# Householder columns: the corrections' place among the matrix-vector products, and VectorE's order, chosen by the number of live blocks

## The chip, the cores and the metric

The program runs on 1 core of one Trainium2 chip. The metric is the device time of one execution in microseconds (us); lower is better. Engines are named as the profile names them: PE is TensorE's matmul, PEld TensorE's weight load, DVE is VectorE, ACT is ScalarE, SP is SyncE.

## What is computed

The reference is a chain of eight residual layers over x. One of them, the third graph layer, needs the eigenvectors of a 512 x 512 symmetric matrix:

```python
def _L2_gnn_ref(features, A, W1, b1, W2, b2):
    deg = jnp.sum(A, axis=0) + jnp.sum(A, axis=1) - jnp.diagonal(A)
    d_inv_sqrt = jnp.where(deg > 0, jax.lax.rsqrt(deg), 0.0)
    L = jnp.diag(deg) - A
    L_norm = d_inv_sqrt[:, None] * L * d_inv_sqrt[None, :]
    _, U = jnp.linalg.eigh(L_norm)
    ...
x = x + _L2_gnn_ref(_layernorm(x, axis=-1), adj, ...)
```

The matrix depends on `adj` alone, so the kernel does this part first: `tridiagonalize` takes the symmetrised matrix to tridiagonal form by 512 Householder reflections, one column after the other. All of the change lies in it. Everything after it (`eigenvectors` and the eight layers) is untouched.

## The kernel before

The 512 columns are cut into 4 phases of 128. In phase `ph` the first `ph` blocks of 128 rows are done, so `L = NB - ph` blocks are live: 4, 3, 2, then 1. All small vectors have 128 partitions and `L` elements in each. A phase has 8 panels of 16 columns (`PW = 16`; `j` counts the columns of a panel). Inside a panel the matrix `A` is not updated; instead each new column gets corrections from the reflectors of the panel so far (`VW`, 2j vectors). At a panel's end two transposes and one rank-32 product on TensorE update `A`, and `A` is split anew into three bf16 parts (`parts`).

One column is a chain between VectorE and TensorE, with a little of ScalarE. With the lines of the profile:

- VectorE writes the new column `x` (L590) and the panel's vector pair (`update_column`, L478).
- `norm_parts`: two sums of products go to TensorE (`part`, L318 and L326, or L328 at one block); `x` is split into three bf16 numbers (R1, L329; R2, L334, which signals `xb_in`); the mask for "is anything nonzero" is multiplied (L331).
- `pair_sums`: the products of the column with the panel's vectors (L414) and their sum over blocks (L421, signals `sums_in`).
- TensorE adds the parts over partitions (`norm_sum`, L680, into `tot`); then it waits for `xb_in` and computes the matrix-vector products `ax` (L702: `3*L*L` matmuls of 128 x 128 by 3, `L` groups of `3*L`), and among them the `corrections` (L691, into `sr`), which wait for `sums_in`. Their place is before group `L // 2`; at one block it is behind the group.
- ScalarE takes the root (L645). VectorE makes the signed norm (L342, L344, L347, `sign_norm` L359), multiplies the corrections out (`spread`, L426) and sums them (`corrected`, L441), then waits for `ax_out`.
- Behind `ax_out`: `sum_parts` (L452), `reflector` (L368), `shifted_column` (L447), `leading` (L375), `product_column` (L458), `inverses` (L382), and the two dot products `jc` and `jd` (L576, L577, or L580, L582 at one block), which go to TensorE (`dots`, L714). While TensorE adds them, VectorE does `inverse_c` (L389), `scales` (L396, L397), `base_column` (L464), `scaled_x` (L404) and `masked_base` (L471). With `dots` the next `x` is written.

VectorE's order is the program's order: each engine takes its instructions one by one, and a wait in front of one holds all behind it. The first column of a panel (j = 0) does its norm ahead, while TensorE updates `A`.

`wide_step` in the listing is never run: it needs `L > 4`, and `L` is at most 4. All columns go through `narrow_step`.

The place of the corrections, in TensorE's program:

```python
for m in range(ph, NB):
    if L > 1 and m == ph + L // 2:
        corrections()
    for b in range(ph, NB):
        for n, A_part in enumerate(parts):
            ins = nc.tensor.matmul(ax[:, m, 0:3], ...)
```

Of the kernel before, what the change touches and what calls it, by code (L numbers as in the profile page):

```python
# [9 lines left out]
ALU = mybir.AluOpType  # L10
ACT = mybir.ActivationFunctionType
AX = mybir.AxisListType
# [63 lines left out]
def tridiagonalize(nc, C, adj_d, adjT_d, V, G, ER, DR, also):  # L76
# [10 lines left out]
    with ExitStack() as ctx:  # L87
# [32 lines left out]
        xax = sb("xax", [P, NB, 3])  # L120
# [3 lines left out]
        prod = sb("prod", [P, 2 + 2 * PAIR, NB])  # L124
        prod2 = sb("prod2", [P, 2, 2, NB, 1 + PAIR])
        sums, srs = sb("sums", [P, 2 + 2 * PAIR]), sb("srs", [P, 2 + 2 * PAIR])
        cross, ab = sb("cross", [P, 2 * PAIR]), sb("ab", [P, 4])
        part, part2 = sb("part", [P, 4]), sb("part2", [P, 1])
# [9 lines left out]
        turned, dots, dots2 = M[0:PAIR, NB - 2, :], M[:, 0, 0:2], M[:, 1, 0:1]  # L138
# [5 lines left out]
        part2_in, dots2_out, mask0, acol0 = sem("part2_in"), sem("dots2_out"), sem("mask0"), sem("acol0")  # L144
# [146 lines left out]
        for ph in range(NB):  # L291
# [3 lines left out]
            split_sums = L > 4  # L295
            SUM0 = 2 if split_sums else 1
            ahead = lambda panel: panel in panels and panel > panels[0]
            with nc.Block() as block:
                @block.vector
                def _(dve):  # L300
# [10 lines left out]
                    def norm_parts(done, j):  # L311
# [3 lines left out]
                        R_1, R_2 = XM[:, q, live, R1], XM[:, q, live, R2]  # L315
# [13 lines left out]
                        V_.tensor_tensor(R_1, x, XB[:, q, live, 2 * XC + 1], ALU.subtract).then_inc(ch, 1)  # L329
                        r1_made = done.next()  # L330
                        V_.scalar_tensor_tensor(prod[:, 0, live], x, 0.0, below, ALU.not_equal, ALU.mult).then_inc(ch, 1)  # L331
                        made["nonzero"] = done.next()
                        dve.wait_ge(ch, r1_made)
                        V_.tensor_tensor(R_2, R_1, XB[:, q, live, 2 * R1 + 1], ALU.subtract).then_inc(xb_in, 1)  # L334

                    def signed_norm(done, j):
# [12 lines left out]
                        if j == 0 or split_sums:  # L349
                            sign_norm(done, j, twice)  # L350
# [55 lines left out]

                    def pair_sums(done, j):

                        q, J = j % 2, 2 * j
                        first, x, below = column(q)  # L410
                        xm = XM[:, q, live, :]
                        if j > 0:
                            dve.wait_ge(ch, made["w"])
                            V_.tensor_tensor(  # L414
                                prod[:, SUM0:SUM0 + 2 * J, live].rearrange("p (h j) b -> p h j b", h=2),
                                VW[:, live, 0:J].rearrange("p b j -> p j b").unsqueeze(1).broadcast_to([P, 2, J, L]),
                                xm[:, :, FIRST:XC + 1].rearrange("p b h -> p h b").unsqueeze(2).broadcast_to([P, 2, J, L]),
                                ALU.mult).then_inc(ch, 1)
                            made["nonzero"] = done.next()
                        dve.wait_ge(ch, made["nonzero"])  # L420
                        V_.tensor_reduce(sums[:, 0:SUM0 + 2 * J], prod[:, 0:SUM0 + 2 * J, live], AX.X, ALU.add).then_inc(sums_in, 1)  # L421

                    def spread(done, j, sums_of):

                        q, J = j % 2, 2 * j
                        V_.tensor_tensor(  # L426
                            prod2[:, q, :, live, 1:1 + J],
                            VW[:, live, PAIR:PAIR + J].unsqueeze(1).broadcast_to([P, 2, L, J]),
                            sums_of.rearrange("p (h j) -> p h j", h=2).unsqueeze(2).broadcast_to([P, 2, L, J]),
                            ALU.mult).then_inc(ch, 1)  # L430
                        made["spread"] = done.next()
# [54 lines left out]
                    def wide_step(done, j, k):  # L486

                        q, J = j % 2, 2 * j
                        first, x, below = column(q)
                        if j > 0:  # L490
                            dve.wait_ge(dots2_out, j)
                            update_column(done, j - 1, dots2)
                        V_.tensor_tensor(prod[:, 1, live], x, A[:, live, k + 1], ALU.mult).then_inc(ch, 1)
                        made["nonzero"] = done.next()
                        pair_sums(done, j)
                        if j > 0 or not made["ahead"]:
                            signed_norm(done, j)
                            leading(done, j)
                            reflector(done, j)
                            inverses(done, j)  # L500
                        dve.wait_ge(sr_out, j + 1)
                        V_.tensor_copy(srs[:, 0:2 + 2 * J], sr[:, 0:2 + 2 * J]).then_inc(ch, 1)
                        held = done.next()
                        dve.wait_ge(ch, held)
                        if j > 0:
                            spread(done, j, srs[:, 2:2 + 2 * J])
                        inverse_c(done, j, srs[:, 0:1])
                        if j > 0:
                            V_.tensor_tensor(
                                cross[:, 0:2 * J].rearrange("p (h i t) -> p h i t", h=2, t=2),  # L510
                                srs[:, 2:2 + 2 * J].rearrange("p (h i t) -> p h i t", h=2, t=2)[:, :, :, ::-1],
# [2949 lines left out]
```

## Time and profile before

| what | us |
|---|---|
| median of 3 runs | 6996.93 (6984.87 to 6997.0) |
| the profiled execution | 6991.48 |
| its span, first to last instruction | 6989.8 |
| first `x` to last `x` of phase L = 4 (128 columns) | 50.14 to 745.30 |
| of L = 3 | 763.83 to 1366.81 |
| of L = 2 | 1380.78 to 1930.51 |
| of L = 1 | 1941.09 to 2457.84 |

The four phases fill the first 35% of the span. On the page PE is busy for 72% of the whole, DVE for 66%, ACT for 33%, but that is a mean over stages of different kinds. The page's chain of what ended last names only the very end (X, L2018). For the columns one reads the timeline of single columns: a line gives start, duration, engine, line, operation, out<-in and, in brackets, how long the engine had been idle and what ended that. "x24" means that so many alike instructions stand in one line.

### The profile page before, as it was taken

What the parts mean: (1) busy time and instruction counts of PE and PEld (TensorE: products, weight loads), DVE (VectorE), ACT (ScalarE), POOL (GpSimd) and SP (SyncE); (2) the same over time, 40 slices, a digit from 0 to 9 for tenths busy, and PEclk for the clock granted to TensorE, in tenths of its full rate; (3) what the DMA queues carried; (4) which work ended last, traced back from release to release, by engine and by line L of the source; (5) the groups of instructions that cost most, each with busy time, mean ns of one, the idle gap of its engine ahead of it and who ended that gap; (6) DMA issues with size and microseconds to landing.
All of it is one profiled execution on the core that took longest, in us unless ns stands there. A gap on an engine that the chain in (4) does not pass through costs nothing. (4 is left out here: it accounts for less than half of the span.)

```text
span 6989.8 us, 107601 instructions
## 1 busy us (share of the span) xinstructions
PE 5054.2 (72%) x32063; PEld 3565.7 (51%) x32063; DVE 4611.9 (66%) x27100; ACT 2308.3 (33%) x7352; POOL 17.9 (0%) x36
## 2 busy tenths in 40 slices
PE   4666555555544479988999995994474699776999
PEld 4555544444433335455666662563242477544676
DVE  7888888888888843248999998677454333424333
ACT  1222222222222234337688994110020133201333
POOL 0000000000000000000000000000000000000000
PEclk9999999999999999988999997997787799886999
DMA  0000000000000000010000000000010000000000
GB/s 37 2 2 2 2 1 1 2 1 1 1 1 1 1 20 0 0 49 7 4 6 4 6 4 8 1 1 1 1 49 1 12 0 0 9 0 13 0 0 24
DMA packets 23206, 48.04 MB, mean 7 GB/s; under 512 B 5673, under 2 KB 16322, under 8 KB 20930
## 3 DMA queue, kind: packets, MB, share of 16 engines
q1 hardware_dynamic: 22722, 42.40, 1.8%
q8 instruction: 204, 3.34, 0.2%
q14 instruction: 280, 2.29, 0.1%
HBM read 34.00 MB, written 8.39 MB: 6 GB/s over the span
## 5 line engine op out<-in xcount | busy, mean ns | idle before, releaser
L714 PE MATMUL h_M<-h_part,ones 128*128 128x2 f32 x1024 | 300.7, 363 | 585.9 <-DVE h_jd L577 422.2
L2011 DVE SCALAR_TENSOR_TENSOR f_ACC<-f_yp,f_CG,f_ACC 128x128 f32<-128x128 f32 x1024 | 288.4, 344 | 461.6 <-DVEq L2009 461.5
L702 PEld LDWEIGHTS h_ax<-h_XM,h_parts 128*128 128x128 bf16 x11520 | 529.7, 117 | 114.0 <-issue 114.0
L714 PEld LDWEIGHTS h_M<-h_part,ones 128*128 128x128 f32 x1024 | 256.7, 311 | 635.6 <-DVE h_jd L577 454.9
L680 PE MATMUL h_tot<-h_part,ones 128*128 128x2 f32 x1024 | 300.8, 363 | 378.7 <-DVE h_jb L326 291.1
L1956 PEld LDWEIGHTS f_yp<-f_W,f_hs 128*128 128x128 f32 x4096 | 490.0, 192 | 92.5 <-issue 91.8
L1890 PE MATMUL f_hp<-f_rows,f_W 128*128 128x512 f32 x1024 | 531.4, 601 | 5.1 <-ACT U L1900 3.0
L1058 ACT ACTIVATE e_XD<-e_X,e_scal 128x60 f32<-128x60 f32 x2048 | 527.6, 333 | 17.5 <-DVEq L922 15.7
L1987 ACT ACTIVATE f_hs<-f_hp,f_b 128x512 f32<-128x512 f32 x512 | 347.6, 685 | 539.6 <-ACTq L1986 539.6
L659 ACT ACTIVATE h_VW<-h_v,h_s 128x8 f32<-128x8 f32 (+3 forms) x512 | 154.8, 302 | 1122.9 <-DVE h_s L396 1122.9
L1946 PE MATMUL f_hp<-f_XT,f_W 128*128 x1024 | 483.5, 600 | 33.0 <-PEq L2240 33.0
L702 PE MATMUL h_ax<-h_XM,h_parts 128*128 128x3 bf16 x11520 | 441.2, 167 | 87.9 <-DVE h_parts L169 87.8
L1956 PE MATMUL f_yp<-f_W,f_hs 128*128 128x128 f32 x4096 | 493.5, 275 | 0.0
L680 PEld LDWEIGHTS h_tot<-h_part,ones 128*128 128x128 f32 x1024 | 256.8, 312 | 438.5 <-DVE h_jb L326 336.4
L1880 PEld LDWEIGHTS f_yp<-f_W,UT 128*128 128x128 f32 x2048 | 266.5, 194 | 188.8 <-issue 92.2
L1880 PEld LDWEIGHTS f_yp<-f_W,U 128*128 128x128 f32 x2048 | 268.5, 192 | 114.2 <-issue 93.1
L691 PE MATMUL h_sr<-h_sums,ones 128*128 128x1 f32 (+15 forms) x1024 | 320.4, 403 | 3.9
L1880 PE MATMUL f_yp<-f_W,UT 128*128 128x128 f32 x2048 | 281.0, 281 | 41.4 <-ACT UT L1900 32.2
L2577 PE MATMUL g_PG<-g_HL,g_Wih 128*128 128x256 f32 (+2 forms) x624 | 288.4, 619 | 1.0 <-DVE g_HL L2524 0.8
L645 ACT ACTIVATE h_s<-h_tot 128x1 f32<-128x1 f32 x512 | 87.8, 171 | 590.2 <-PE h_tot L680 589.6
L943 DVE SCALAR_TENSOR_TENSOR e_PB<-e_PB,e_scal,e_u 128x60 f32<-128x60 f32 x1024 | 281.2, 275 | 0.1
L947 DVE SCALAR_TENSOR_TENSOR e_PB<-e_PB,e_scal,e_u 128x60 f32<-128x60 f32 x1024 | 281.2, 275 | 0.0
(685 smaller groups left out, 10601.6 us busy)
## 6 DMA issues: line engine op xcount, KB each, us to landing
f_S<-in_f_W SPq DMA_DIRECT2D x64, 128.0 KB, 2.2
X<-in_x SPq DMA_DIRECT2D x1, 4096.0 KB, 16.3
f_W<-in_f_W SPq DMA_DIRECT2D x2, 2048.0 KB
spill<-f_xts SPq DMA_DIRECT2D x16, 256.0 KB, 2.0
f_rows<-spill SPq DMA_DIRECT2D x16, 256.0 KB, 2.6
f_W<-in_f_W SPq DMA_DIRECT2D x4, 1024.0 KB
out<-X SPq DMA_DIRECT2D x1, 4096.0 KB, 11.1
h_A<-in_adj SPq DMA_DIRECT2D x1, 1024.0 KB, 5.5
```

What stands on the lines that cost most here:

```text
L680: nc.tensor.matmul(tot[j % 2][:, 0:2], C.ones[:, :], part[:, 0:2], start=True, stop=True).then_inc(tot_out, 1)
L691: nc.tensor.matmul(sr[:, 0:n], C.ones[:, :], sums[:, 0:n], start=True, stop=True).then_inc(sr_out, 1)
L702: ins = nc.tensor.matmul(ax[:, m, 0:3], A_part[:, b, m * P:(m + 1) * P], XB[:, q, b, 2 * XC + 1:2 * R2 + 2:2], start=(b == ph and n == 0), ...
L714: nc.tensor.matmul(dots, C.ones[:, :], part[:, 2:4], start=True, stop=True).then_inc(dots_out, 1)
L1058: ins = nc.scalar.activation(XD[b][:, k, h, :], X[:, :], ACT.Identity, bias=scal[b][:, k, 2 * h:2 * h + 1])
L1880: ins = nc.tensor.matmul(self.yp[d % 3][:, 0:D], self.hs[unit % 2][:, j, i * P:(i + 1) * P], self.W2[:, unit % E * FC + j, :], start=(j == ...
L1890: nc.tensor.matmul(self.hp[s % 3][:, :], self.W1[:, e, j * P:(j + 1) * P], self.rows[:, g % 2, :], start=True, stop=True).then_inc(self.h_ ...
L1946: nc.tensor.matmul(hp[:, u % 2, c, :], W1[:, col // F, col % F:col % F + P], rows_t, start=True, stop=True).then_inc(h_full, 1)
L1956: ins = nc.tensor.matmul(yp[:, u % 2, k, :], hs[:, u % 2, c, k * P:(k + 1) * P], W2[:, u * UC + c, :], start=(c == 0), stop=(c == UC - 1))
L1987: nc.scalar.activation(hs[:, u % 2, c, :], hp[:, u % 2, c, :], func, bias=b1[:, u * UC + c:u * UC + c + 1]).then_inc(hs_full, 1)
L2011: ins = V_.scalar_tensor_tensor(ACC[:, k, :], yp[:, u % 2, k, :], CG[:, k * E + e:k * E + e + 1], ACC[:, k, :], ALU.mult, ALU.add)
L2577: ins = nc.tensor.matmul(o2, Wih[:, p - 1, gi * D:(gi + 1) * D], x, start=True, stop=(t == 0))
```

## The change

- `wide_step` and all that only it used go away, with two semaphores (`dots2_out`, `part2_in`) that were cleared at each panel's end on VectorE and TensorE.
- The corrections move: at L = 4 from behind two groups of products to behind one; at L = 3 and 2 from behind one to ahead of all; at L = 1 from behind the only one to ahead of it.
- `narrow = L <= 3` now names widths 3, 2 and 1. There VectorE makes the pair products and their sums before the third part R2 of `x`, and `reflector` stands before the wait for `ax_out`.
- At L = 4 `sign_norm` stands before the wait for the corrections; `leading`, `reflector`, `shifted_column` and `inverses` before the wait for `ax_out`; `inverse_c` before `jc` and `jd`.
- At the first column of a panel the sums are made with the norm ahead.

```diff
-            split_sums = L > 4
-            SUM0 = 2 if split_sums else 1
+            narrow = L <= 3
...
+                    def opening(done, j):
+                        norm_parts(done, j)
+                        if narrow:
+                            nonzeros(done, j)
+                            if j > 0:
+                                pair_products(done, j)
+                            first_rest(done, j)
+                            pair_sums(done, j)
+                            second_rest(done, j)
+                        else:
+                            first_rest(done, j)
+                            nonzeros(done, j)
+                            second_rest(done, j)
+                            if j > 0:
+                                pair_products(done, j)
+                            pair_sums(done, j)
...
+                    def norm_ahead(done):
+                        opening(done, 0)
+                        sign_norm(done, 0, signed_norm(done, 0))
+                        leading(done, 0)
+                        reflector(done, 0)
+                        inverses(done, 0)
...
+                        fresh = j > 0 or not made["ahead"]
+                        if fresh:
+                            opening(done, j)
                             twice = signed_norm(done, j)
+                            if not narrow or j == 0:
+                                sign_norm(done, j, twice)
                         dve.wait_ge(sr_out, j + 1)
                         if j > 0:
-                            spread(done, j, sr[:, 1:1 + 2 * J])
-                            sign_norm(done, j, twice)
+                            spread(done, j)
+                            if narrow:
+                                sign_norm(done, j, twice)
                         corrected(done, j)
-                        dve.wait_ge(ax_out, j + 1)
-                        sum_parts(done)
-                        if j > 0 or not made["ahead"]:
-                            reflector(done, j)
-                        shifted_column(done, j)
-                        if j > 0 or not made["ahead"]:
-                            leading(done, j)
-                        product_column(done)
-                        if j > 0 or not made["ahead"]:
-                            inverses(done, j)
+                        if narrow:
+                            if fresh:
+                                reflector(done, j)
+                            dve.wait_ge(ax_out, j + 1)
+                            sum_parts(done)
+                            shifted_column(done, j)
+                            if fresh:
+                                leading(done, j)
+                            product_column(done)
+                            if fresh:
+                                inverses(done, j)
+                        else:
+                            if fresh:
+                                leading(done, j)
+                                reflector(done, j)
+                            shifted_column(done, j)
+                            if fresh:
+                                inverses(done, j)
+                            dve.wait_ge(ax_out, j + 1)
+                            sum_parts(done)
+                            inverse_c(done, j, sr[:, 0:1])
+                            product_column(done)
...
-                        inverse_c(done, j, sr[:, 0:1])
+                        if narrow:
+                            inverse_c(done, j, sr[:, 0:1])
...
-                        for used in (ch, masks_in, dots_out, dots2_out, sr_out, root_out, ax_out, scaled_out, kept):
+                        for used in (ch, masks_in, dots_out, sr_out, root_out, ax_out, scaled_out, kept):
...
-                                if L > 1 and m == ph + L // 2:
+                                if m == (ph if narrow else ph + 1):
                                     corrections()
...
-                            if L == 1:
-                                corrections()
...
-                        for used in (panel_in, part_in, part2_in, sums_in, xb_in):
+                        for used in (panel_in, part_in, sums_in, xb_in):
```

`first_rest` is R1, `second_rest` is R2, `nonzeros` is L331, `pair_products` is L414 and `pair_sums` is now L421 alone.

## Rows read from the trace of the kernel before

**Rows 1.** Windows of L = 4 and L = 1: start:end, length, busy us of engines, PEclk, DMA share.

```profile
50.14:745.30 695.16, 436.64 (x6970) 374.66 (x6970) 560.33 (x4268) 148.79 (x825) 0.00 (x0) 1.00 0.01 2
1941.09:2457.84 516.75, 243.83 (x1171) 204.95 (x1171) 438.99 (x3825) 112.55 (x783) 0.00 (x0) 1.00 0.00 1
```

**Rows 2.** Timeline, one column of L = 4, j = 3.

```profile
238.90 0.86 PEld L702 LDWEIGHTS h_ax<-h_XM,h_parts 128*128 128x128 bf16 x24
239.02 0.21 DVE L421 TENSOR_REDUCE h_sums<-h_prod 128x13 f32<-128x52 f32 x1
...
239.64 0.23 DVE L347 SCALAR_TENSOR_TENSOR h_s<-h_s,h_tot 128x1 f32<-128x1 f32 x1
239.68 0.50 PEld L691 LDWEIGHTS h_sr<-h_sums,ones 128*128 128x128 f32 x2
...
239.92 0.90 PEld L702 LDWEIGHTS h_ax<-h_XM,h_parts 128*128 128x128 bf16 x24
240.13 0.78 PE L702 MATMUL h_ax<-h_XM,h_parts 128*128 128x3 bf16 x24
240.32 0.20 DVE L426 TENSOR_TENSOR h_prod<-h_VW,h_sr 128x48 f32<-128x48 f32 x1 [0.46 <-PE h_sr L691]
...
240.56 0.21 DVE L441 TENSOR_REDUCE h_zy<-h_prod 128x8 f32<-128x56 f32 x1
240.95 0.17 DVE L452 TENSOR_REDUCE h_y<-h_ax 128x4 f32<-128x12 f32 x1 [0.17 <-PE h_ax L702]
241.03 0.21 DVE L368 SCALAR_TENSOR_TENSOR h_v<-h_XM,h_s 128x4 f32<-128x4 f32 x1
241.17 0.21 DVE L447 SCALAR_TENSOR_TENSOR h_zc<-h_zy,h_s 128x4 f32<-128x4 f32 x1
...
241.61 0.16 DVE L576 SCALAR_TENSOR_TENSOR h_jc<-h_XM,h_pc 128x4 f32<-128x4 f32 x1
...
241.92 0.59 PE L714 MATMUL h_M<-h_part,ones 128*128 128x2 f32 x2 [1.01 <-DVE h_jd L577]
...
242.63 0.23 DVE L590 SCALAR_TENSOR_TENSOR h_XM<-h_vm,h_M,h_base 128x4 f32<-128x4 f32 x1
```

**Rows 3.** Timeline, one column of L = 4, j = 10.

```profile
271.68 0.33 DVE L421 TENSOR_REDUCE h_sums<-h_prod 128x41 f32<-128x164 f32 x1
...
272.12 0.50 PEld L691 LDWEIGHTS h_sr<-h_sums,ones 128*128 128x128 f32 x2
...
274.10 0.16 DVE L576 SCALAR_TENSOR_TENSOR h_jc<-h_XM,h_pc 128x4 f32<-128x4 f32 x1
```

**Rows 4.** Timeline, one column of L = 3, j = 8.

```profile
947.53 0.16 DVE L329 TENSOR_TENSOR h_XM<-h_XM 128x3 f32<-128x3 f32 x1
...
948.10 0.26 DVE L421 TENSOR_REDUCE h_sums<-h_prod 128x33 f32<-128x99 f32 x1
...
948.41 0.50 PEld L691 LDWEIGHTS h_sr<-h_sums,ones 128*128 128x128 f32 x2
...
949.55 0.16 DVE L452 TENSOR_REDUCE h_y<-h_ax 128x3 f32<-128x9 f32 x1
...
950.20 0.16 DVE L576 SCALAR_TENSOR_TENSOR h_jc<-h_XM,h_pc 128x3 f32<-128x3 f32 x1
```

**Rows 5.** Timeline, one column of L = 2, j = 15.

```profile
1577.24 0.28 DVE L421 TENSOR_REDUCE h_sums<-h_prod 128x61 f32<-128x122 f32 x1
...
1577.57 0.50 PEld L691 LDWEIGHTS h_sr<-h_sums,ones 128*128 128x128 f32 x2
```

**Rows 6.** Timeline, one column of L = 1, j = 3.

```profile
2019.26 0.23 DVE L347 SCALAR_TENSOR_TENSOR h_s<-h_s,h_tot 128x1 f32<-128x1 f32 x1
2019.46 0.17 DVE L426 TENSOR_TENSOR h_prod<-h_VW,h_sr 128x16 f32<-128x16 f32 x1
```

**Rows 7.** Timeline, the end of a panel of L = 4.

```profile
120.83 0.23 DVE L478 SCALAR_TENSOR_TENSOR h_VW<-h_VW,h_M,h_pc 128x8 f32<-128x8 f32 x1
121.68 1.41 PEld L720 LDWEIGHTS h_M<-ident,h_VW 128*32 128x32 f32 x8 [1.21 <-issue]
```

More of the change, by code:

```diff
@@ L405, in scaled_x, with pair_products, spread @@
                         made["vm"] = done.next()
-                    def pair_sums(done, j):
[L409 to L423, printed above, removed]
+                    def pair_products(done, j):
+                        J = 2 * j
+                        xm = XM[:, j % 2, live, :]
+                        dve.wait_ge(ch, made["w"])
+                        V_.tensor_tensor(
+                            prod[:, 1:1 + 2 * J, live].rearrange("p (h j) b -> p h j b", h=2),
+                            VW[:, live, 0:J].rearrange("p b j -> p j b").unsqueeze(1).broadcast_to([P, 2, J, L]),
+                            xm[:, :, FIRST:XC + 1].rearrange("p b h -> p h b").unsqueeze(2).broadcast_to([P, 2, J, L]),
+                            ALU.mult).then_inc(ch, 1)
+                        made["prod"] = done.next()
+                    def pair_sums(done, j):
+                        dve.wait_ge(ch, made["prod"])
+                        V_.tensor_reduce(sums[:, 0:1 + 4 * j], prod[:, 0:1 + 4 * j, live], AX.X, ALU.add).then_inc(sums_in, 1)
+                    def spread(done, j):
                         q, J = j % 2, 2 * j
@@ L551, in narrow_step @@
-                    def narrow_step(done, j, k):
-                        q, J = j % 2, 2 * j
-                        first, x, below = column(q)
-                        pair_sums(done, j)
-                        twice = None
-                        if j > 0 or not made["ahead"]:
+                    def opening(done, j):
[14 more added lines that the diff above has]
+                            pair_sums(done, j)
@@ L563, in narrow_step @@
                         corrected(done, j)
-                        dve.wait_ge(ax_out, j + 1)
-                        sum_parts(done)
-                        if j > 0 or not made["ahead"]:
-                            reflector(done, j)
-                        shifted_column(done, j)
-                        if j > 0 or not made["ahead"]:
-                            leading(done, j)
-                        product_column(done)
-                        if j > 0 or not made["ahead"]:
-                            inverses(done, j)
+                        if narrow:
[20 more added lines that the diff above has]
+                            product_column(done)
@@ L613, in _ @@
                         if made["ahead"]:
[L614 to L618 removed]
+                            norm_ahead(done)
                         sp = ph if panel + 1 in panels else ph + 1
```

112 lines of the change are left out of this document (23 added, 89 removed).

## Prediction

> **What bounds the kernel now.** I read the windows by phase first, then the timeline of single columns at each width and each j, and last the panel's end. The windows show what kind of stage this is: VectorE is busy for 560 of 695 us at four blocks and for 439 of 517 at one, TensorE for 437 and 244, and the granted clock is 1.00, the upper level of 2.4 GHz, in both, also where TensorE idles for half the time [rows 1]. So neither engine's total is the bound. A column is one chain that goes from VectorE to TensorE and back three times, and 512 columns stand one behind the other: 2408 of 6990 us lie there, and what a column's chain gains, the kernel gains. Nothing else runs beside it.
>
> In the column of L = 4, j = 3 the reader is to see three things [rows 2]. TensorE takes up the corrections (239.68) only when its 24 weight loads are through; the sums that they need were ready at 239.02 + 0.21 = 239.23. VectorE waits twice: 0.46 us for the corrections, and 0.17 us for the products (240.95). And behind the products there are six starts up to `jc` at 241.61, of which only `sum_parts`, `product_column` and `jc` need the products.
>
> The steps that I use, all from these rows. A short VectorE instruction starts 0.08 behind another that it doesn't need (240.95, 241.03) and 0.14 behind one with a column and a per-partition scalar (241.03, 241.17); behind a wide one it may start about 0.08 before that one's end. One that needs the result starts 0.04 after its end (240.32 + 0.20, then 240.56) [rows 2]. TensorE starts 0.05 after the VectorE instruction that it waits for (1577.24 + 0.28, then 1577.57) [rows 5]. A weight load of the products takes 0.78/24 = 0.0325, the corrections hold TensorE for 0.24 (239.68 to 239.92), and their result is used 0.64 after their start (240.32) [rows 2].
>
> **Dead code.** `wide_step` never ran, so its removal is worth nothing but one semaphore clear less per panel on each engine. VectorE's lies beside TensorE's transposes. TensorE's lies on the path: from the end of L478 (121.06) to the transposes (121.68) there are 0.62 us with five clears in them [rows 7]. Less the 0.05 of the wake-up that is 0.11 a clear at most, 0 at least; I take 0.1, since nothing else is in the gap: 32 panels, 3 us.
>
> **L = 4, early columns (j = 3).** The corrections stand behind 12 loads, so they start at 238.90 + 0.39 = 239.29 (the sums are there at 239.28), 0.39 earlier. TensorE doesn't stand, so the products end where they did, and `sum_parts` stays at 240.95. VectorE has `sign_norm` done ahead (239.64 + 0.23 + 0.04 = 239.91), so `spread` starts at 239.99, `corrected` 0.24 later at 240.23, and `leading`, `reflector`, `shifted_column`, `inverses` at 240.36, 240.44, 240.58, 240.72, all covered by the wait for the products. Then `inverse_c` at 241.03, `product_column` at 240.95 + 0.17 + 0.04 = 241.16, `jc` 0.16 + 0.04 later at 241.36 instead of 241.61: 0.25. At the column's end TensorE's `dots` end at 241.92 + 0.59 = 242.51, so x could start at 242.55, but did at 242.63 [rows 2]: `inverse_c` made VectorE's own chain the later one. With it moved ahead the `dots` are last, another 0.08. Together 0.33; in the sum I use 0.32 for j = 1 to 3.
>
> **L = 4, late columns.** The sums grow with j. At j = 10 they are there at 271.68 + 0.33 + 0.05 = 272.06, so the corrections start only 0.06 before the 272.12 of now [rows 3], TensorE stands from the 12th load until then, and 12 more loads (0.39) are left behind them: the products end 0.33 later. VectorE is no earlier: `spread` at 272.75 (0.64 and 0.05 for the wider result, an estimate), `corrected` at 273.11, as wide as the sum, the four moved ones at 273.36, 273.44, 273.58 and 273.72, `sum_parts` at 273.80 and `jc` 0.40 later, 274.20 against 274.10 [rows 3]; less the 0.08 at the end it is even. From j = 11 on VectorE itself is the later one, and the column loses 0.03 to 0.09. Between j = 3 and 10 the gain falls in a line with the sums: 0.26, 0.23, 0.18, 0.14, 0.10, 0.07, 0.01. A panel: 0.94 + 0.99 - 0.35 = 1.58, and the first column, whose reflector is made ahead anyhow, gives 0.2 (`inverse_c` and `shifted_column` off the two tails; an estimate from the same steps). 8 panels: 14.3 us.
>
> **L = 3, 2, 1: the price.** R2, which starts the matrix loads, now stands behind the pair products and their sum. At L = 3, j = 8: `nonzeros` takes R1's place (947.53), the products start at 947.61, take 0.26 (as wide as the sum), R1 at 947.78, the sum at 947.91, R2 at 948.08, TensorE at 948.08 + 0.17 + 0.05 = 948.30. The corrections so start 0.11 before the 948.41 of now, but all 27 loads stand behind them: 948.30 + 0.24 + 0.88 and some 0.25 for the last matmul to end give `sum_parts` at 949.71 against 949.55. Behind it `reflector` is gone: `jc` at 949.71 + 0.08 + 0.25 + 0.20 = 950.24 against 950.20 [rows 4]. A loss of 0.04. With few vectors (j = 1, 2) R2 is early and the column gains 0.05; with many (j = 11 to 15) VectorE was late for the products anyhow and gains 0.05 to 0.11. A panel: 0.40, and 0.05 for the first column; 8 panels: 3.6 us.
>
> **L = 2 and 1: the gain.** Here the matrix loads are 12 and 3, and what ends last is the corrections. At L = 2, j = 15 the products and the sum come 0.20 earlier (two starts are moved behind them), the sum at 1577.04, R2 at 1577.24, TensorE at 1577.46 instead of 1577.57: 0.11, which stays to the end of the column, for VectorE has the same instructions behind it [rows 5]. In the first columns the root chain takes its place: at L = 1, j = 3 `spread` can't start before 2019.26 + 0.14 = 2019.40, against 2019.46, and `reflector`, now before the products' wait, is held by `sign_norm` for as much [rows 6]; nothing is left there (at j = 1 a loss of 0.08). By the same steps for each j: 1.22 a panel at L = 2 and 0.75 at L = 1, with first columns (0.05 and 0.08) 10.2 and 6.6 us.
>
> **Costs that the trace doesn't show.** The new neighbours on VectorE (R2 behind a reduction, `reflector` behind one) have no row. From below, a start 0.08 behind the one before; from above, 0.04 after its end, some 0.2 later at these widths [rows 2, 4]. I take the overlap, since it is what independent neighbours show, and keep 0.05 a column either way for the range: 384 columns, 19 us.
>
> One rule speaks against this. The Trainium skill ("VectorE: DVE Perf Modes", the section on the DRAIN) says that the next VectorE instruction doesn't start before the pipe is empty, and advises to count instructions, not semaphores; as the change leaves their number as it is, the order at L = 3 to 1 would bring only delay of R2. The trace disagrees: 0.08 from start to start at a duration of 0.17.
>
> **The sum.** 14.3 + 3.6 + 10.2 + 6.6 + 3 = 37.7 us off the profiled execution's 6991.5: 6953.8. The median stands 5.4 above that execution, so 6959.
>
> **Rivals.**
> - *Only L = 4 gains.* If R2 comes some 0.08 later than reckoned at the small widths, their 20 us go. What is left is 14.3 + 3 and little more: 6979. For it: every column of L = 3 from j = 4 to 8 is reckoned at a small loss already. Against it: L = 2 and 1 have slack for the products.
> - *Slower: R2 held for full durations.* If each of the products and the sum holds VectorE to its end, R2 at L = 3, j = 8 starts at 947.61 + 0.26 + 0.16 + 0.26 = 948.29, 0.21 later than reckoned. In L = 3 that adds 0.21 to the 11 columns that wait for the products and half of it to the others, 2.3 a panel less: 18 us lost. At L = 2 and 1 corrections start 0.1 later than now: 12 and 10 us lost. With 17 + 2 gained elsewhere the kernel is 21 us slower, 7018. It decides from about 0.1 later per column of L = 3 to 1. Against it: the starts 0.08 apart [rows 2]. The page named above would have it so.
> - *L = 4 keeps its gain to the end of the panel.* If VectorE overlaps more behind the wide sums than by 0.08, the columns j = 8 to 15 gain 0.2 each instead of nothing (14 us in 8 panels), and the others 0.03 (2 us): 6943. For it: the late columns are reckoned as VectorE's alone. Against it: no row shows a larger overlap.
> - *Nothing measurable.* The sums reach TensorE later than the 0.05 of now because both engines meet there at each width: 0.07 for each of 512 columns takes the whole. For it speaks only that it is small; 6990.
>
> **How the numbers follow.** The forecast has 0.67, only L = 4 0.11, the slower case 0.06, the larger gain 0.08, nothing measurable 0.08. The range goes from 6940 (the 19 us of the unknown starts below; the larger gain lies in it) to 6981 (most of the same above; L = 4 alone lies in it). This kernel can be told from no change from about 0.2% on, 14 us. Faster by that: 0.67 + 0.08 and most of 0.11, 0.83; within it 0.11; slower 0.06.
>
> **What would show it.** In the changed trace: at L = 4, j = 3 the corrections' load 0.39 behind the first matrix load and not 0.78, VectorE's wait before `spread` under 0.1 instead of 0.46, `jc` 0.40 behind `sum_parts` instead of 0.66, and x to x 0.33 shorter; at j = 10 x to x as now. At L = 3, j = 8 R2 0.55 behind `nonzeros`, and `sum_parts` still waiting for the products. At L = 2, j = 15 x to x 0.10 shorter. The forecast is wrong if R2 at L = 3, j = 8 comes later than 0.65 behind `nonzeros`, if TensorE's clock falls below 1.00 in a phase, or if time moves outside the four phases.

## The result and the profile after

| | before | after |
|---|---|---|
| median of 5 runs each | 6994.21 us (6984.87 to 6997.0) | 6952.92 us (6928.83 to 6955.84) |
| ratio, 95% interval | | 0.9936 [0.9923, 0.995] |
| the profiled execution, its span | 6991.48, 6989.8 | 6955.57, 6953.9 |
| first `x` to last `x`, L = 4 | 695.16 | 681.44 |
| L = 3 | 602.98 | 592.77 |
| L = 2 | 549.73 | 538.38 |
| L = 1 | 516.75 | 508.40 |
| first `x` of all to the last | 2407.70 | 2363.86 |

The changed kernel is faster by 0.64%. The columns gained 43.84 us; the gaps between the phases gave 0.2 of it. Below, "the columns" is always this stretch, from the first `x` to the last. It is the cleaner measure, because what stands behind the last `x` doesn't repeat as well: two executions of the changed kernel differ by 2.6 us in the columns and by 32 us behind them (the last experiment). By their times its five executions fall into two groups, one at 6928.83 and four at 6952.63 to 6955.84.

The windows of the four phases in the changed kernel (start:end, length, then busy us of PE, PEld, DVE, ACT and POOL, the granted clock, DMA share, GB/s; the first and the last are to be set beside [rows 1]):

```profile
49.85:731.29 681.44, 445.54 (x6970) 378.61 (x6970) 562.86 (x4268) 148.89 (x824) 0.00 (x0) 1.00 0.01 2
749.61:1342.38 592.77, 351.75 (x4275) 302.57 (x4275) 501.51 (x4248) 133.40 (x811) 0.00 (x0) 1.00 0.01 2
1356.12:1894.50 538.38, 280.55 (x2342) 244.25 (x2342) 457.03 (x4226) 121.47 (x797) 0.00 (x0) 1.00 0.00 1
1905.31:2413.71 508.40, 236.44 (x1171) 206.34 (x1171) 427.64 (x3824) 112.53 (x783) 0.00 (x0) 1.00 0.00 1
```

The instructions are as many as before and the clock is 1.00, the upper level, throughout. VectorE's busy time at L = 4 is even 2.5 us longer, while the phase is 13.7 us shorter; at L = 1 it is 11.4 us shorter, because overlapping instructions count once there: the sum of VectorE's single durations changed by 2 us or less in each phase. So, but for one semaphore clear less at each panel's end, nothing was made cheaper: the gain is order and place.

One column of L = 4, j = 3 (to be set beside [rows 2]; start, duration, engine, line, operation; in brackets the idle time before and what ended it):

```profile
233.60 0.23 DVE L574 SCALAR_TENSOR_TENSOR h_XM<-h_vm,h_M,h_base 128x4 f32<-128x4 f32 x1 [0.20 <-PE h_M L682]
...
234.47 0.54 PEld L677 LDWEIGHTS h_ax<-h_XM,h_parts 128*128 128x128 bf16 x12
...
234.94 0.50 PEld L666 LDWEIGHTS h_sr<-h_sums,ones 128*128 128x128 f32 x2
...
235.55 0.16 DVE L365 TENSOR_TENSOR h_s<-h_s 128x1 f32<-128x1 f32 x1
235.62 0.20 DVE L433 TENSOR_TENSOR h_prod<-h_VW,h_sr 128x48 f32<-128x48 f32 x1
...
236.52 0.17 DVE L459 TENSOR_REDUCE h_y<-h_ax 128x4 f32<-128x12 f32 x1
...
236.93 0.17 DVE L559 SCALAR_TENSOR_TENSOR h_jc<-h_XM,h_pc 128x4 f32<-128x4 f32 x1
...
237.24 0.59 PE L682 MATMUL h_M<-h_part,ones 128*128 128x2 f32 x2 [0.75 <-DVE h_jd L560]
...
237.93 0.23 DVE L574 SCALAR_TENSOR_TENSOR h_XM<-h_vm,h_M,h_base 128x4 f32<-128x4 f32 x1 [0.20 <-PE h_M L682]
```

The corrections' load (L666) now stands 0.47 behind the first matrix load (L677), not 0.78, and `spread` (L433) follows `sign_norm` (L365) by 0.07, so the 0.46 of wait is gone. Of the two waits that [rows 2] show on VectorE, the one for the products has shrunk from 0.17 to 0.05 (`inverses` ends at 236.47). What is left besides is 0.21 for ScalarE's root, ahead of L350 at 235.02, and 0.20 ahead of x, for the `dots` (L682).

One column of L = 3, j = 8 (to be set beside [rows 4]):

```profile
928.77 0.23 DVE L574 SCALAR_TENSOR_TENSOR h_XM<-h_vm,h_M,h_base 128x3 f32<-128x3 f32 x1
...
929.22 0.16 DVE L341 SCALAR_TENSOR_TENSOR h_prod<-h_XM 128x3 f32<-128x3 f32 x1
929.30 0.26 DVE L418 TENSOR_TENSOR h_prod<-h_VW,h_XM 128x96 f32<-128x96 f32 x1
...
929.47 0.16 DVE L329 TENSOR_TENSOR h_XM<-h_XM 128x3 f32<-128x3 f32 x1
929.59 0.26 DVE L428 TENSOR_REDUCE h_sums<-h_prod 128x33 f32<-128x99 f32 x1
929.76 0.15 DVE L336 TENSOR_TENSOR h_XM<-h_XM 128x3 f32<-128x3 f32 x1
929.97 0.50 PEld L666 LDWEIGHTS h_sr<-h_sums,ones 128*128 128x128 f32 x2
...
930.21 1.01 PEld L677 LDWEIGHTS h_ax<-h_XM,h_parts 128*128 128x128 bf16 x27
...
930.42 0.89 PE L677 MATMUL h_ax<-h_XM,h_parts 128*128 128x3 bf16 x27
...
931.34 0.17 DVE L459 TENSOR_REDUCE h_y<-h_ax 128x3 f32<-128x9 f32 x1
...
931.87 0.16 DVE L559 SCALAR_TENSOR_TENSOR h_jc<-h_XM,h_pc 128x3 f32<-128x3 f32 x1
```

R1 (929.47) and R2 (929.76) each start while the wide instruction ahead of them (L418 until 929.56, L428 until 929.85) still runs. R2 ends last, at 929.91, and TensorE starts 0.06 behind it. `sum_parts` (L459) still waits for the products: it starts 0.03 behind the end of the last matmul (931.31). One column of L = 2, j = 15 (to be set beside [rows 5]):

```profile
1479.48 0.23 DVE L574 SCALAR_TENSOR_TENSOR h_XM<-h_vm,h_M,h_base 128x2 f32<-128x2 f32 x1
1480.31 0.28 DVE L428 TENSOR_REDUCE h_sums<-h_prod 128x61 f32<-128x122 f32 x1
1480.50 0.15 DVE L336 TENSOR_TENSOR h_XM<-h_XM 128x2 f32<-128x2 f32 x1
1480.71 0.50 PEld L666 LDWEIGHTS h_sr<-h_sums,ones 128*128 128x128 f32 x2 [0.15 <-DVE h_XM L336]
...
1483.60 0.23 DVE L574 SCALAR_TENSOR_TENSOR h_XM<-h_vm,h_M,h_base 128x2 f32<-128x2 f32 x1
```

The corrections come 1.23 after x; in the kernel before they came 1.36 after it (1577.57 [rows 5]), whose x is this row:

```profile
1576.21 0.23 DVE L590 SCALAR_TENSOR_TENSOR h_XM<-h_vm,h_M,h_base 128x2 f32<-128x2 f32 x1
```

The column takes 4.12 against a median of 4.26 before. And one column of L = 1, j = 3 (to be set beside [rows 6]):

```profile
1979.00 0.22 DVE L355 SCALAR_TENSOR_TENSOR h_s<-h_s,h_tot 128x1 f32<-128x1 f32 x1
1979.14 0.16 DVE L433 TENSOR_TENSOR h_prod<-h_VW,h_sr 128x12 f32<-128x12 f32 x1
1979.33 0.16 DVE L365 TENSOR_TENSOR h_s<-h_s 128x1 f32<-128x1 f32 x1
1979.52 0.22 DVE L374 SCALAR_TENSOR_TENSOR h_v<-h_XM,h_s 128x1 f32<-128x1 f32 x1
```

`spread` starts 0.14 behind the root's last step (L355), and `reflector` (L374) waits for `sign_norm` (L365): the root is the limit here. The median column takes 3.75 against 3.70 before.

The medians of x to x for each j, gain in us:

| | j = 0 | 1 | 3 | 5 | 8 | 10 | 12 | 15 |
|---|---|---|---|---|---|---|---|---|
| L = 4 | 0.27 | 0.29 | 0.28 | 0.28 | 0.13 | 0.01 | -0.11 | -0.11 |
| L = 3 | 0.14 | 0.12 | 0.08 | 0.03 | 0.02 | 0.06 | 0.12 | 0.13 |
| L = 2 | 0.20 | 0.01 | -0.01 | 0.06 | 0.14 | 0.14 | 0.14 | 0.13 |
| L = 1 | 0.20 | -0.05 | -0.05 | 0.00 | 0.08 | 0.14 | 0.13 | 0.14 |

### The profile page after: what moved, and what is told of

Its sections match the earlier page's. It is cut to its first block and busy times, and to the rows that moved or that the text cites. A ratio compares the mean times of both kernels' runs of the same rounds, so it can differ in the third digit from the quotient of the medians.

```text
span 6953.9 us, 107895 instructions
## 1 busy us (share of the span) xinstructions
PE 5069.5 (73%) x32063; PEld 3580.7 (51%) x32063; DVE 4581.1 (66%) x27100; ACT 2308.4 (33%) x7352; POOL 17.9 (0%) x36
## 5 line engine op out<-in xcount | busy, mean ns | idle before, releaser
L682 PE MATMUL h_M<-h_part,ones 128*128 128x2 f32 x1024 | 300.4, 363 | 523.1 <-DVE h_jd L560 358.5
L682 PEld LDWEIGHTS h_M<-h_part,ones 128*128 128x128 f32 x1024 | 256.3, 311 | 566.8 <-DVE h_jd L560 391.3
L677 PEld LDWEIGHTS h_ax<-h_XM,h_parts 128*128 128x128 bf16 x11520 | 480.9, 114 | 40.9 <-issue 40.9
L677 PE MATMUL h_ax<-h_XM,h_parts 128*128 128x3 bf16 x11520 | 407.8, 167 | 30.0 <-DVE h_parts L167 30.0
L666 PE MATMUL h_sr<-h_sums,ones 128*128 128x1 f32 (+15 forms) x1024 | 314.6, 397 | 79.8 <-DVE h_parts L167 57.8
L666 PEld LDWEIGHTS h_sr<-h_sums,ones 128*128 128x128 f32 x1024 | 256.6, 311 | 112.7 <-issue 72.8
L911 DVE SCALAR_TENSOR_TENSOR e_PB<-e_PB,e_scal,e_u 128x60 f32<-128x60 f32 x1024 | 281.3, 275 | 0.1
```

Of the source, the lines that this page charges most:

```text
L666: nc.tensor.matmul(sr[:, 0:n], C.ones[:, :], sums[:, 0:n], start=True, stop=True).then_inc(sr_out, 1)
L677: ins = nc.tensor.matmul(ax[:, m, 0:3], A_part[:, b, m * P:(m + 1) * P], XB[:, q, b, 2 * XC + 1:2 * R2 + 2:2], start=(b == ph and n == 0), ...
L682: nc.tensor.matmul(dots, C.ones[:, :], part[:, 2:4], start=True, stop=True).then_inc(dots_out, 1)
```

## The experiments

Each kernel computes the whole reference. The gain of each in the columns, against the kernel before, in us (minus is a loss):

| kernel | L = 4 | L = 3 | L = 2 | L = 1 | columns |
|---|---|---|---|---|---|
| the change | 13.7 | 10.2 | 11.4 | 8.4 | 43.8 |
| order only | 3.5 | -5.2 | -3.1 | 3.2 | -1.4 |
| place only | -14.5 | -27.9 | -6.4 | -5.3 | -53.8 |
| R2 first | 14.1 | -12.7 | -5.9 | -5.6 | -9.8 |
| inverse behind (L = 4) | 11.0 | 10.1 | 11.3 | 8.8 | 41.5 |
| corrections ahead of R2's wait | 14.2 | 21.3 | 19.1 | 15.8 | 70.6 |
| the same, orders by column | 18.6 | 21.5 | 20.3 | 17.7 | 78.5 |
| the change again | 14.2 | 11.0 | 11.9 | 9.1 | 46.5 |
| R2 first, own wait | 14.0 | -2.2 | 3.8 | 4.3 | 20.2 |

**Order only, place only.** Is it VectorE's order or the place of the corrections? The first kernel puts the corrections back behind the groups where they stood; the second keeps their new place and puts VectorE's old order back (the diffs are against the changed kernel).

```diff
-                                if m == (ph if narrow else ph + 1):
+                                if L > 1 and m == ph + L // 2:
                                     corrections()
...
+                            if L == 1:
+                                corrections()
```

> VectorE's new order at every width, the corrections where they were before. Theory (both halves are needed): at L = 4 VectorE's four moved instructions no longer fit ahead of the products, since the corrections come 0.3 to 0.4 later than in the changed kernel: x to x at j = 3 about 4.42 (before 4.62, changed 4.33), at j = 10 about 4.74, so the phase keeps some 6 us of the 14 that the change gained there. At L = 3 the late R2 delays the first loads and the corrections behind them: x to x at j = 8 about 4.3 (before 4.15), the phase 18 us slower than before; L = 2 some 10 us slower, L = 1 about even. In all some 20 us slower than before, 7015. Rival (VectorE's order alone brings the gain, the corrections' place is idle): every phase as in the changed kernel, 6953.

```diff
-                        if narrow:
+                        if False:
                             nonzeros(done, j)
...
-                            if narrow:
-                                sign_norm(done, j, twice)
+                            sign_norm(done, j, twice)
...
                             dve.wait_ge(ax_out, j + 1)
                             sum_parts(done)
+                            if fresh:
+                                reflector(done, j)
```

> The corrections at their new places, VectorE's order in the columns as before. Theory: at L = 4, j = 1 to 4 nothing is gained (VectorE still waits for the products and has all six starts behind them: x to x 4.62), and from j = 5 on TensorE stands and the products come later: 4.9 at j = 10, 5.15 at j = 15, the phase 16 us slower than before. At L = 3 the corrections wait for sums that come behind R2, and all 27 loads behind them: 4.39 at j = 8 (before 4.15), the phase 22 us slower. At L = 2 and 1 the corrections were held by the sums already, so nothing changes (within 2 us each). In all some 34 us slower, 7028. Rival (the place alone brings the gain): L = 4 and the others as in the changed kernel, 6953.

Order only: 6984.35 us (6967.88 to 7004.84), ratio 0.9995 [0.998, 1.0011]: no difference. In the columns it lost 1.4 us where a loss of some 20 was expected. The directions held at L = 3 and 2, the sizes are a third of those expected (-5.2 and -3.1); L = 4 kept 3.5 us where 6 was expected, and L = 1 gained 3.2 where it was to be even. Place only: 7027.57 us, ratio 1.0062 [1.0041, 1.0082], slower, with -14.5 and -27.9 us at L = 4 and 3. So neither half gains anything alone over all columns, and the change is not the sum of its halves: at the small widths the new place pays only once the sums are early, and the early sums pay fully only if TensorE takes them up early; at L = 4 the new place pays only with VectorE's new order behind it. What I had not reckoned is the loss of place only at L = 2 and 1 (0 was expected, -6.4 and -5.3 measured). One column of it, L = 3, j = 8, shows where it comes from:

```profile
1050.57 0.26 DVE L428 TENSOR_REDUCE h_sums<-h_prod 128x33 f32<-128x99 f32 x1
1050.94 0.50 PEld L653 LDWEIGHTS h_sr<-h_sums,ones 128*128 128x128 f32 x2 [0.30 <-issue]
```

The sums end at 1050.83 and TensorE starts 0.11 later, not 0.05 as in [rows 5], and its idle time is put down to "issue". In all 360 columns of L = 3 to 1 with j above 0 this delay is 0.114 to 0.117 here, against a median of 0.054 in the kernel before. In this place the corrections' wait for the sums stands directly behind the wait for R2, and TensorE idles in both. That this pair of waits is the cause is tested below (R2 first, own wait).

**R2 first.** The changed kernel, but with R1 and R2 ahead of the pair products at L = 3 to 1, as before. This is the rival of the held R2, taken from the other side: it prices what the sums gain from going first.

```diff
                     def opening(done, j):
                         norm_parts(done, j)
-                        if narrow:
+                        if False:
```

> The changed kernel, but at L = 3, 2 and 1 VectorE makes R1 and R2 ahead of the pair products, as before. Theory (sums first is the gain there, as the corrections wait for the sums and all loads for the corrections): corrections start when the sums end, at L = 3, j = 8 1.33 after x instead of 1.20, x to x 4.27 instead of 4.13; L = 3 loses 14 us against the changed kernel, L = 2 9, L = 1 5, L = 4 nothing; 28 us in all, 6978 to 6980. Rival (the late R2 costs more than the early sums give): L = 3 faster than in the changed kernel, below 590 us from first x to last.

7007.11 us (6978.35 to 7009.99), ratio 1.0019 [1.0007, 1.003]; the columns are 53.6 us behind the changed kernel, twice the expected. One column of L = 3, j = 8:

```profile
935.52 0.23 DVE L574 SCALAR_TENSOR_TENSOR h_XM<-h_vm,h_M,h_base 128x3 f32<-128x3 f32 x1
...
936.54 0.26 DVE L428 TENSOR_REDUCE h_sums<-h_prod 128x33 f32<-128x99 f32 x1
...
936.91 0.50 PEld L666 LDWEIGHTS h_sr<-h_sums,ones 128*128 128x128 f32 x2 [0.30 <-issue]
```

The sums start 1.02 after x instead of 0.82, for two instructions stand ahead of the products again, and the corrections 1.39 instead of 1.20. Here too they are 0.11 behind the sums' end (936.80). So the change needs the new order on VectorE at the small widths, and the rival that R2 would be held is out: at L = 3 R2 is 0.54 behind `nonzeros`.

**Inverse behind.** `inverse_c` at L = 4 behind `jc` and `jd` again, to price the tail of the column.

```diff
-                            inverse_c(done, j, sr[:, 0:1])
                             product_column(done)
...
-                        if narrow:
-                            inverse_c(done, j, sr[:, 0:1])
+                        inverse_c(done, j, sr[:, 0:1])
```

> The changed kernel, with inverse_c at L = 4 behind jc and jd again. Theory (the 0.08 at the column's end): x comes 0.93 and not 0.85 behind jd's start, jc where it was, so every column of L = 4 is 0.08 longer, the phase 10 us, some 691.5 from first x to last instead of 681.4; the other phases unchanged. Rival (the dots end the column in any case): no change at L = 4.

One execution: L = 4 takes 684.19 us, 2.75 longer than in the changed kernel, where 10 was expected (the changed kernel's own two executions differ by 0.5 there); the column j = 3 takes 4.36 instead of 4.33. The tail is worth 0.03 a column, not 0.08.

**Corrections ahead of R2's wait, and orders by column.** If two waits in a row are dear and R2 is what TensorE waits for at L = 3, the corrections don't need R2: their wait can go first. The second kernel adds, by column, the order that was the better one there.

```diff
+                            if narrow:
+                                corrections()
                             pe.wait_ge(xb_in, j + 1)
...
-                                if m == (ph if narrow else ph + 1):
+                                if not narrow and m == ph + 1:
```

> The changed kernel, but at 3, 2 and 1 live blocks TensorE's corrections stand ahead of its wait for the second rest (xb_in) instead of behind it. Theory (a wait that stands directly behind another wait holds TensorE 0.11 us from the sums' end only if the second wait is the later one; here each wait has an instruction of its own, and the 0.50 us of the corrections' load starts with the sums, not with R2, that is about 0.07 us earlier at 3 live blocks, j=8: 1.13 us after x where the changed kernel has 1.20): about 0.07 us a column wherever the matrix products end last (3 blocks), and wherever the corrections do (2 and 1 blocks late in the panel): 8 us at 3 blocks, 5.6 at 2, 2.8 at 1, together some 16 us of the columns off the changed kernel, so about 6936 us. Rival (R2 and the products that wait for it are the limit, so the corrections merely come earlier and the matrix products where they were): nothing at 3 blocks, 2 to 3 us at 2 and 1, 6950. Rival on the other side (the corrections' semaphore and switch are paid twice, because TensorE idles a second time ahead of xb_in): R2 is 0.17 us behind the sums and the load lasts 0.50, so it doesn't idle; if it did, +0.05 a column, 16 us slower.

```diff
-                                if not narrow and m == ph + 1:
+                                if not narrow and m == ph + (1 if j <= 10 else 2):
...
+                        late = not narrow and j > 10
+                        if late or (L <= 2 and 0 < j <= 5):
+                            dve.wait_ge(ax_out, j + 1)
+                            sum_parts(done)
+                            if fresh:
+                                reflector(done, j)
...
```

> The kernel of the corrections ahead of the wait for R2, and in addition each order only where its columns gained: at 4 live blocks the order of the kernel before (corrections behind two groups, VectorE's old order) for j above 10, where the changed kernel lost 0.06 to 0.11 us a column (5 columns x 8 panels x 0.1 = 4 us), and at 2 and 1 live blocks, j = 1 to 5, the reflector behind the parts' sum as before, where the changed kernel lost or gained 0.00 to 0.05 a column (5 x 16 x 0.025 = 2 us). Theory (each column is a race of its own between sums and products, so the orders can be mixed by column without loss): about 6 us off the kernel of the corrections ahead, near 6930. Rival (the loss late in the panel at 4 blocks is not from the place of the corrections, or a switch of orders inside a panel costs): no difference from that kernel, or up to 3 us slower.

The first takes 6904.21 us (6899.55 to 6921.62), ratio 0.989 [0.9873, 0.9906]; the second 6892.5 us (6889.77 to 6913.77), ratio 0.9875 [0.9856, 0.9893]. Both beat the changed kernel, which took 6938.35 beside them. In the columns that is 24.1 us and another 7.9. A column of the first, L = 3, j = 8:

```profile
925.17 0.23 DVE L574 SCALAR_TENSOR_TENSOR h_XM<-h_vm,h_M,h_base 128x3 f32<-128x3 f32 x1
...
925.99 0.26 DVE L428 TENSOR_REDUCE h_sums<-h_prod 128x33 f32<-128x99 f32 x1
926.16 0.15 DVE L336 TENSOR_TENSOR h_XM<-h_XM 128x3 f32<-128x3 f32 x1
926.30 0.50 PEld L666 LDWEIGHTS h_sr<-h_sums,ones 128*128 128x128 f32 x2
926.54 1.01 PEld L679 LDWEIGHTS h_ax<-h_XM,h_parts 128*128 128x128 bf16 x27
```

The corrections start 1.13 after x, as expected, 0.05 behind the sums, and the products follow with no gap: R2 was through (926.31) before the corrections let TensorE go. The surprise is in the first columns, which I had not counted: they gained 0.42, 0.42 and 0.57 each at L = 3, 2 and 1, in seven panels of each phase, together some 10 of the 24.1 us. A first column of L = 1, in the changed kernel and then in this one:

```profile
2160.57 0.29 DVE L167 TENSOR_TENSOR h_parts<-h_left,h_parts 128x128 bf16<-128x128 f32 x1 [0.38 <-ACT h_parts L158]
2161.11 0.50 PEld L666 LDWEIGHTS h_sr<-h_sums,ones 128*128 128x128 f32 x2 [2.60 <-issue]
...
2161.91 0.15 DVE L459 TENSOR_REDUCE h_y<-h_ax 128x1 f32<-128x3 f32 x1
```

```profile
2136.04 0.50 PEld L666 LDWEIGHTS h_sr<-h_sums,ones 128*128 128x128 f32 x2 [0.23 <-issue]
...
2137.87 0.29 DVE L167 TENSOR_TENSOR h_parts<-h_left,h_parts 128x128 bf16<-128x128 f32 x1 [0.38 <-ACT h_parts L158]
...
2138.42 0.16 PEld L679 LDWEIGHTS h_ax<-h_XM,h_parts 128*128 128x128 bf16 x3 [1.87 <-issue]
...
2138.70 0.16 DVE L459 TENSOR_REDUCE h_y<-h_ax 128x1 f32<-128x3 f32 x1 [0.30 <-PE h_ax L679]
```

In the changed kernel the corrections wait, with the products, for the panel's last split (L167) and then go first, so `sum_parts` comes 1.05 behind that split's end. Here they start 2.1 us before it ends, and `sum_parts` comes 0.54 behind it.

The orders by column gave 4.4 us at L = 4 (each j above 10 is back within 0.01 of the kernel before), 1.2 at L = 2 and 1.9 at L = 1: 7.9 with the 0.2 at L = 3, where 6 were expected.

**R2 first, own wait.** Is the 0.11 from the two waits, or from VectorE's order? R2 first again, with the corrections' wait ahead of R2's.

```diff
+                            if narrow:
+                                corrections()
                             pe.wait_ge(xb_in, j + 1)
...
```

> The kernel with R2 ahead of the pair products at 3, 2 and 1 live blocks (whose corrections started 0.11 us behind the end of the sums, as the second of two waits in a row), with the corrections' wait for the sums put ahead of the wait for R2, an instruction of its own. Theory (two waits in a row, of which the second is the late one, cost TensorE 0.06 us more than one): corrections 0.05 us behind the sums' end, 1.33 us after x at 3 live blocks, j=8, where R2 first had 1.39; with 0.06 us on some 300 columns and 0.4 to 0.55 us on each of 24 first columns that is some 28 us off the columns of R2 first, so 17 us less than the kernel before from first x to last x; and the kernel with the corrections ahead of the wait and the sums first stays some 55 us ahead of it, because the order on VectorE is worth 0.20 us a column either way. Rival (the 0.11 us belongs to VectorE's order: a sum that stands right behind the products it needs signals later): corrections still 0.11 us behind the sums' end, and only the first columns gain, 11 us.

```profile
932.42 0.23 DVE L574 SCALAR_TENSOR_TENSOR h_XM<-h_vm,h_M,h_base 128x3 f32<-128x3 f32 x1
...
933.43 0.26 DVE L428 TENSOR_REDUCE h_sums<-h_prod 128x33 f32<-128x99 f32 x1
933.74 0.50 PEld L666 LDWEIGHTS h_sr<-h_sums,ones 128*128 128x128 f32 x2 [0.23 <-DVE h_sums L428]
```

The sums end at 933.69 and TensorE starts at 933.74: 0.05 with the same order on VectorE. In all 360 columns the delay is 0.051 to 0.054, where R2 first has 0.114 to 0.117. The columns, of one execution, are 20.2 us better than before (17 expected) and 30 better than R2 first (28 expected), of which some 10 lie in the first columns. The kernel with the sums first and the corrections ahead of R2's wait stays 50.3 ahead of this one. So both are shown: two waits in a row cost 0.06 us a column, and the sums' place is worth some 50 us by itself.

**The change again**, beside the last two on the same chip.

> The changed kernel once more, beside the two others on the same chip. Theory (the change moves the columns alone, by 43.8 us, and the rest of the kernel has two outcomes some 21 us apart, by the clock granted in the stretch behind the panels, that the change does not touch): columns again 2363.9 us from the first x to the last, within 0.5; ratio to the kernel before between 0.991 and 0.996. Rival (the change itself lowers the clock later, through more work in less time): the stretch behind the panels at 198 us again, as in the first profile, in every execution.

6938.35 us (6921.25 to 6953.89), ratio 0.9937 [0.9916, 0.9959]. The columns took 2361.22, 2.6 less than the first time (0.5, 0.7, 0.6 and 0.8 in the four phases), more than the 0.5 that I expected. From the last `x` to the end it took 4508.4 us against 4540.2, and most of the difference is one stretch late in the program. Its windows, first in the changed kernel's first execution (the whole stretch and its last quarter), then in this one:

```profile
6090.50:6289.00 198.50, 154.83 (x464) 100.01 (x464) 49.19 (x161) 16.14 (x35) 0.00 (x0) 0.77 0.00 0
6240.00:6289.00 49.00, 36.10 (x113) 29.32 (x111) 10.30 (x23) 0.03 (x1) 0.00 (x0) 0.67 0.00 0
```

```profile
6078.00:6255.00 177.00, 133.35 (x464) 82.32 (x464) 49.15 (x161) 16.12 (x35) 0.00 (x0) 0.87 0.00 0
6210.00:6255.00 45.00, 28.75 (x152) 24.08 (x152) 12.96 (x29) 0.01 (x1) 0.00 (x0) 1.00 0.00 0
```

The matmuls are as many (x464); in the last quarter the clock is 1.00, the upper level of 2.4 GHz, in the second execution, and 0.67 in the first, a mean between the two levels of 1.2 and 2.4 GHz. Some 8 of the other 10 us lie in the first 240 us behind the last `x`: in the 60 us from 2443 on the first execution's clock was 0.89, then 0.83, and in the second execution's 60 us from 2440 on it was 1.00, then 0.94.

The kernel before took 197.0 us in the late stretch, at 0.78, so it is long without the change, and long or short with it: the rival, that the change brings the clock down in every execution, falls. That the change has no part in it is not shown, though. With the stretch shorter by 21.5 us the profiled execution of the kernel before, 6991.48, would be at 6970; its 31 executions in this record took 6978.95 to 6997.2, and none is that short, while three of the nine of the changed kernel are (6921.25 to 6928.83, the others 6950.11 to 6955.84). What decides it is open.

## Why the prediction was right, and where it was not

The forecast was 6959 and the median is 6952.9. The sum of 37.7 us stands against 43.8 in the columns (46.5 in the second execution) and 41.3 between the medians. What is measured for a phase below holds its share of the panel ends too, about 0.8 us of the 3 reckoned for dead code. By the steps of the sum:

- **Dead code.** At a panel's end of L = 4 in the changed kernel:

```profile
118.99 0.23 DVE L485 SCALAR_TENSOR_TENSOR h_VW<-h_VW,h_M,h_pc 128x8 f32<-128x8 f32 x1
119.73 1.41 PEld L688 LDWEIGHTS h_M<-ident,h_VW 128*32 128x32 f32 x8 [1.07 <-issue]
```

  From 119.22 to 119.73 are 0.51 where there were 0.62 [rows 7] (medians of the 32 panel ends: 0.50 and 0.62): 0.11 for the one clear less, 0.1 was taken. With it the first columns, reckoned at 0.15 to 0.3 a panel clears included, gained 0.14 to 0.27.
- **L = 4, early.** 14.3 was reckoned for the phase (1.78 a panel, which is 14.2), 13.7 and 14.2 measured. That they agree is partly luck, for the parts of a panel miss both ways: by the medians of each j the columns 1 to 3 gained 0.86 (0.94 reckoned), 4 to 10 gained 1.21 (0.99), 11 to 15 lost 0.48 (0.35), and the first gained 0.27 (0.3 with the clear). `jc` is 0.41 behind `sum_parts` (0.40 reckoned) and `spread` doesn't wait. The mis-sized term is the tail: x to x is 0.29 shorter, not 0.33, and the inverse-behind kernel prices the tail at 0.03, not 0.08. The step that failed is "x could start at 242.55": I let VectorE start 0.04 behind the modelled end of the `dots`, but where it clearly waits for them, it starts 0.10 behind it (237.24 + 0.59 = 237.83, x at 237.93). The corrections' load came 0.47 behind the first matrix load, not 0.39, which cost nothing: `spread` follows `sign_norm`, not the corrections.
- **L = 4, late.** j = 10 gained 0.01, as reckoned; j = 11 to 15 lost 0.06 to 0.11, where 0.03 to 0.09 was said. The rival that the gain holds to the panel's end is out. That the old order is better there is shown by the kernel with orders by column.
- **L = 3.** 3.6 was reckoned and 10.2 measured: the one large miss. Nearly every step held: R2 0.54 behind `nonzeros` (0.55), the corrections 1.20 after x (1.22), `jc` 0.53 behind `sum_parts` (0.53). But the matrix loads start 0.24 behind the corrections and `sum_parts` 1.13 behind their start (931.34 - 930.21), where I had 0.88 for the loads, 0.25 for the last matmul and 0.04 on top, 1.17. The rows have 0.21 from the first load to the first matmul, 0.89 for the matmuls and 0.03 on top, so the term that was mis-sized is the 0.25, for which the prediction names no row. It and the corrections' 0.02 are 0.06 a column, which on 120 columns is the miss (5.8 us without the phase's share of dead code). At a loss of 0.04 reckoned at j = 8 the sign hung on it: the columns j = 5 to 8 gained 0.02 to 0.03.
- **L = 2 and 1.** 10.2 and 6.6 were reckoned, 11.4 and 8.4 measured. The corrections of L = 2, j = 15 come 0.13 earlier, with 0.11 reckoned, and that stays to the column's end (0.13). Early in the panel the root is the limit, as said; at L = 1, j = 3 it costs 0.05, where the working left nothing.
- **The unknown starts.** The overlap was right: R2 0.17 behind the start of a sum that lasts 0.26, R1 0.17 behind the products' start. What the Trainium skill says ("VectorE: DVE Perf Modes", the section on the DRAIN), that the next instruction doesn't start before the pipe is empty, and which would have made the change slower, is not seen at these neighbours: they start 0.09 before the end of the instruction ahead of them (929.47 against 929.56, 929.76 against 929.85). The same section ends the rule with "A next op that is not held starts earlier"; the prediction left that out, and earlier starts are what the rows show.
- **What lay outside the sum.** The sum took the rest of the kernel as unchanged. Behind the last `x` it was 8.2 us longer in the first execution of the changed kernel and 23.6 shorter in the second. By my own list, time that moves outside the phases makes the forecast wrong. As it moves both ways with the same kernel, it is no fixed price of the change, but whether the change has a part in it is open (the last experiment). That the median came within 6 us of the forecast is partly luck: the columns gave 6 us more than the sum, and four of the five executions behind the median had the long rest; the fifth, 6928.83, lies below the range of 6940 to 6981.

## What to carry to other kernels

Where two engines hand one chain back and forth, order and place must be priced together: VectorE's new order and the corrections' new place were each worth nothing or less alone (-1.4 and -53.8 us) and 43.8 together. Look at what a waiting instruction really needs: the corrections were tied to a wait for R2 that they did not need, and taking them out of it was worth another 24 us, two fifths of it in the first columns, where the wait was for a whole panel's update. And where a sum of small steps decides a sign over hundreds of columns, read each step from a row; two steps too long by 0.02 and 0.04 were some 6 us here.

## What the runs showed of the hardware

- TensorE started 0.05 to 0.06 us behind the VectorE instruction that it waited for, but 0.11 when that wait stood directly behind another one that was met first (936.80 to 936.91 in R2 first, against 933.69 to 933.74 with a wait of its own). In the profile the 0.11 reads "issue", while the 0.05 of that own wait names the instruction.
- A short VectorE instruction that doesn't need the result started 0.09 before the end of the wide one ahead of it (R1 at 929.47, R2 at 929.76 in the changed kernel).
- The same stretch of 464 matmuls took 177 us in one execution of the changed kernel and 198.5 in another, at mean granted clocks of 0.87 and 0.77, and 197.0 at 0.78 in the kernel before.
